# Spreading Bx with two single-pass products, moving the second group of flips, and moving half of the Bx products, in an adapter-plus-experts kernel

## The reference

```
Bx    = einsum('bni,bri->bnr', x, B[itok])          # 512 x 16 per batch
c     = einsum('bnr,bor->bno', Bx, A[itok])         # adapter output
base  = c @ base_w.T + base_b
w     = top2(softmax(c @ router_w.T)), renormalised
delta = einsum('bse,bsr,eor->bso', w, c @ A.T, B)   # 16 experts, rank 64
out   = x + base + 0.5 * delta
```

## Time and profile before

| | before |
|---|---|
| median of 3 runs | 446.18 us |
| lowest and highest | 445.64, 464.56 us |
| the profiled execution | 445.62 us, of it 443.8 us span |
| TensorE busy | 92% of the span |
| VectorE busy | 72% |
| ScalarE busy | 24% |
| GpSimd busy | 9% |
| granted TensorE clock | 0.996 of full speed |

### The profile page before, as it was taken

The page is one execution under the profiler, slowest core; times in us unless marked ns, Lnnn a source line. Parts: engine busy times, 40 slices in busy tenths (PEclk is TensorE's granted clock), DMA queues, the critical chain, the costliest instruction groups (busy, mean ns, idle before and its releaser), DMA issues.

```text
span 443.8 us, 6785 instructions
## 1 busy us (share of the span) xinstructions
PE 409.7 (92%) x2496; PEld 279.9 (63%) x2496; DVE 319.4 (72%) x830; ACT 108.1 (24%) x163; POOL 40.5 (9%) x53
## 2 busy tenths in 40 slices
PE   0597997999788999999999999999999999999996
PEld 0475985656556766666667666666666676666665
DVE  2699996999468496668677875966686778756453
ACT  0003114435473231123113112311231131123110
POOL 4020000002100120012001201200120012012000
PEclk9999998999999999999999999999999999999999
DMA  8999999999999999899999999998999898556935
GB/s 223 357 330 331 334 357 366 345 269 336 289 295 239 352 362 323 279 349 342 310 287 378 306 315 302 366 312 295 348 335 325 285 366 303 207 201 217 343 128 189
DMA packets 75027, 135.35 MB, mean 305 GB/s; under 512 B 5506, under 2 KB 14770, under 8 KB 74994
## 3 DMA queue, kind: packets, MB, share of 16 engines
q1 hardware_dynamic: 56000, 102.08, 69.7%
q10 hardware_dynamic: 18994, 32.84, 23.5%
HBM read 99.23 MB, written 35.65 MB: 304 GB/s over the span
## 4 chain that ended last, share of the span: by engine, by line
PE 63%; DVE 10%; DMA 9%; SPq 6%; POOL 3%; ACT 3%; issue 3%; ACTq 2%; POOLq 0%; DVEq 0%
PE ps L927 13%; PE ps L928 11%; PE ps L929 11%; PE ps L901 11%; PE ps L941 6%; DMA bexpT<-in_x 6%; PE ps L930 5%; POOL u_r L480 3%; DMA gm_r<-xT 3%; DVE xT L728 3%; DVE early L659 3%; SPq L296 3%; ACT bexpT L495 2%; PE ps L856 2%; PE ps L949 2%
## 5 line engine op out<-in xcount | busy, mean ns | idle before, releaser
L840 DVE TENSOR_TENSOR xbuf<-ps,xbuf 128x512 f32<-128x512 f32 x128 | 86.7, 677 | 96.0 <-PE ps L930 96.0
L927 PE MATMUL ps<-h_r,u_r 128*128 128x512 f32 x256 | 108.8, 425 | 0.7
L928 PE MATMUL ps<-h_r,u_r 128*128 128x512 f32 x256 | 100.3, 392 | 0.0
L929 PE MATMUL ps<-h_r,u_r 128*128 128x512 f32 x256 | 100.1, 391 | 0.0
L866 PE MATMUL ps<-early 128*128 128x256 f32 x256 | 66.5, 408 | 22.6 <-DVE early L659 22.6
L728 DVE STREAM_TRANSPOSE xT<-xbuf 128x256 f32<-128x256 f32 x224 | 80.6, 410 | 0.0
L866 PEld LDWEIGHTS ps<-early 128*128 128x128 f32 x256 | 48.1, 201 | 36.8 <-issue 16.5
L927 PEld LDWEIGHTS ps<-h_r,u_r 128*128 128x128 f32 x256 | 48.1, 188 | 35.9 <-issue 16.7
L659 DVE STREAM_TRANSPOSE early<-xbuf 128x256 f32<-128x256 f32 x128 | 65.9, 577 | 5.3 <-issue 3.8
L901 PE MATMUL ps<-bexpT,cur 128*32 128x512 f32 x512 | 61.6, 598 | 2.2 <-DVE h_r L707 1.5
L495 ACT ACTIVATE h_r<-ps 128x512 fp32r<-128x512 f32 x64 | 36.2, 595 | 78.8 <-PE ps L901 78.4
(11 more groups left out here) (67 smaller groups left out, 205.3 us busy)
## 6 DMA issues: line engine op xcount, KB each, us to landing
out<-xbuf SPq DMA_DIRECT2D x31, 1024.0 KB, 7.3
xbuf<-in_x SPq DMA_DIRECT2D x28, 1024.0 KB, 7.4
xbuf<-in_x ACTq DMA_DIRECT2D x32, 512.0 KB, 10.9
xbuf<-in_x SPq DMA_DIRECT2D x32, 512.0 KB, 8.6
xbuf<-in_L_ffn_base_w SPq DMA_DIRECT2D x16, 512.0 KB, 19.3
xbuf<-in_L_ffn_base_w ACTq DMA_DIRECT2D x16, 512.0 KB, 20.1
gm_r<-g_hilo SPq DMA_DIRECT2D x128, 32.0 KB, 6.8
early_u<-in_L_ffn_B SPq DMA_DIRECT2D x10, 256.0 KB, 18.5
```

The lines of the kernel that those rows point to most:

```text
L840: dve.tensor_tensor(xs, ps[:, tile_bank(b.n, m), :], xs, ALU.add).then_inc(s_out, 1)
L927: pe.matmul(acc, u_r[:, b.q, 0, h, tok_t], hi, start=(h == 0), stop=False)
L928: pe.matmul(acc, u_r[:, b.q, 0, h, tok_t], lo, start=False, stop=False)
L929: pe.matmul(acc, u_r[:, b.q, 1, h, tok_t], hi, start=False, stop=False)
```

## The change

Four edits, and one argument of the compiler:

1. The spread of Bx. `spread` is float32r, and Bx is split into a high part `bxs_r[:,0]` (a second ScalarE copy out of `BXB` in slot 8) and a low part `bxs_r[:,1]` (a VectorE subtraction, the first thing in slot 9). Two single-pass products replace the one in 32 bits. They stand in slot 10, behind tile 10, and so do ScalarE's copies of the result.
2. Both groups of flips stand behind tile 13. The multiplications that use them stay in slots 13 and 14.
3. The first half of the Bx products stands ahead of tile 4, directly behind `h_products`, for every front (before: ahead of tile 3, with f = 1 already there).
4. `T_AT` changes: in slot 3 nothing, in slots 4, 5, 6 and 7 two pairs each (four transposes). Before it was two pairs in slot 3, two in 4, one in 5, two in 6, one in 7.
5. `dynamic_dma_scratch_size=1024` makes room for the new tile.

```
-        BX_AFTER = {90: 3, 101: 8}
+        BX_AFTER = {90: 4, 101: 8}
...
-        T_AT = {0: (5, 6), 1: (7,), 3: (8, 9), 4: (10, 11), 5: (12,), 6: (13, 14), 7: (15,)}
+        T_AT = {0: (5, 6), 1: (7,), 4: (8, 9), 5: (10, 11), 6: (12, 13), 7: (14, 15)}
...
-            return {4 if f.n == 1 else 3: range(0, KD), 8: range(KD, 2 * KD)}.get(m, ())
+            return {4: range(0, KD), 8: range(KD, 2 * KD)}.get(m, ())
...
-        CT_AT = UP_AT = {13: 0, 14: 1}
+        REP_AT, CT_AT = 10, 13
+        UP_AT = {13: 0, 14: 1}
...
                     copy(bxp, ps[:, BXB, :]).then_inc(s_bxp, 1)
+                    need(act, s_rep, f.n)
+                    copy(bxs_r[:, 0, :], ps[:, BXB, :]).then_inc(s_bxhi, 1)
...
-                if m == SPREAD_AT:
+                if m == REP_AT:
                     act.wait_ge(s_rep, f.n + 1)
...
                 if m == MAX_AT:
+                    dve.wait_ge(s_bxp, f.n + 1)
+                    dve.wait_ge(s_bxhi, f.n + 1)
+                    dve.tensor_tensor(bxs_r[:, 1, :], bxp, f32(bxs_r[:, 0, :]), ALU.subtract).then_inc(s_bxlo, 1)
                     dve.wait_ge(s_lg, f.n + 1)
...
-                    pe.matmul(ps[:, BXB, :], spread[:, f.q, :], bxp,
-                              start=True, stop=True).then_inc(s_rep, 1)
-                if m in CT_AT:
...
+                if m == REP_AT:
+                    pe.wait_ge(s_bxhi, f.n + 1)
+                    pe.wait_ge(s_bxlo, f.n + 1)
+                    pe.matmul(ps[:, BXB, :], spread[:, f.q, :], bxs_r[:, 0, :], start=True, stop=False)
+                    pe.matmul(ps[:, BXB, :], spread[:, f.q, :], bxs_r[:, 1, :], start=False, stop=True)\
+                      .then_inc(s_rep, 1)
+                if m == CT_AT:
                     pe.wait_ge(s_combk, f.n * 2 + 2)
...
-    nc = bacc.Bacc("TRN2", target_bir_lowering=False, num_devices=1)
+    nc = bacc.Bacc("TRN2", target_bir_lowering=False, num_devices=1, dynamic_dma_scratch_size=1024)
```

More of the change, by code:

```diff
@@ L116, in adaln_ffn @@
         ident = sb("ident", [P, P])
-        spread = sb("spread", [P, 2, P])
+        spread = sb("spread", [P, 2, P], F32R)
+        bxs_r = sb("bxs_r", [P, 2, T], F32R)
         pick = sb("pick", [P, 2, RK])
@@ L178, in adaln_ffn @@
         s_xe, s_bxq = sem("x_transposed"), sem("bx_products")
+        s_bxhi, s_bxlo = sem("bx_partial_hi"), sem("bx_partial_lo")
         s_bxp, s_lg, s_rep, s_bx = sem("bx_partial"), sem("logits"), sem("bx_spread"), sem("bx_copied")
@@ L265, in adaln_ffn, with bx_before @@
         T_AHEAD = {12: (0,), 13: (1,), 14: (2,), 15: (3, 4)}
-        T_AT = {0: (5, 6), 1: (7,), 3: (8, 9), 4: (10, 11), 5: (12,), 6: (13, 14), 7: (15,)}
+        T_AT = {0: (5, 6), 1: (7,), 4: (8, 9), 5: (10, 11), 6: (12, 13), 7: (14, 15)}
         REFILL_AT = {4: 0, 8: 1}
-        def bx_before(f, m):
-            return {4 if f.n == 1 else 3: range(0, KD), 8: range(KD, 2 * KD)}.get(m, ())
+        def bx_before(m):
+            return {4: range(0, KD), 8: range(KD, 2 * KD)}.get(m, ())
         def ring_place(f, j):
@@ L933, in bx_products @@
             def bx_products(f, m):
-                for k in bx_before(f, m):
+                for k in bx_before(m):
                     g, j = k // KD, k % KD
@@ L951, in slot @@
                     ins.then_inc(s_lg, 1)
-                    pe.matmul(ps[:, BXB, :], spread[:, f.q, :], bxp,
-                              start=True, stop=True).then_inc(s_rep, 1)
-                if m in CT_AT:
-                    h = CT_AT[m]
-                    pe.wait_ge(s_combk, f.n * 2 + 2)
[L957 to L962, removed]
+                if m == REP_AT:
[5 more added lines that the diff above has]
+                if m == CT_AT:
+                    pe.wait_ge(s_combk, f.n * 2 + 2)
+                    for h in range(2):
+                        if h == 1:
+                            pe.wait_ge(s_bx, f.n + 1)
+                        for t in range(NT):
+                            w = combk[:, t, h * EH:(h + 1) * EH, :].rearrange("p e k -> p (e k)")
+                            ins = flip((MISC, BXB)[h], t * P, w)
+                        ins.then_inc(s_ct, 1)
             pe.wait_ge(s_masks, 4)
```

## The result

The changed kernel takes 448.61 us in the median of 7 runs (447.69 to 450.61). The kernel before takes 445.64 us in the median of 7. The ratio is 1.0072 with a 95% interval of 1.0051 to 1.0094: slower by 0.7%. That is less than 2%, and the interval leaves out 1. Forecast were 449.1 us, range 444.8 to 452.2. Some executions, whatever the kernel, are disturbed and some per cent longer (one of before at 464.56 us), and the ratios leave them out, as do the medians of the experiments' table.

The account below looks back on a forecast made before the run. TensorE was taken as the bound, unless VectorE's stream is longer between meeting points. Six steps of 0.88 - 0.34 (+3.2), step 0 (-0.34) and the first part (+0.6) add 3.5 to 445.62: 449.1 us, range 444.8 to 452.2.

Parts of the forecast that it names:

- The stretch: VectorE's gapless work from tile 4's add to the last transpose ahead of tile 8: from 7.62 to 8.98 us.
- Tile 8: Its start in steps with f = 2 to 7: 0.88 us later, the 0.46 us saved by the Bx move included.
- The spread: Two single-pass products replace the long one: -0.95 + 0.15 + 0.46 = -0.34 us a step, bounds -0.49 and -0.29.
- The term without a row: First product of tile 10, now behind the logits' short products: 0.15 us extra, bounds nothing and 0.20.
- The cover of the subtraction: Slot 9: the 0.67 us subtraction hides in VectorE's 2.08 us idle ahead of tile 10's add, costing nothing.
- Flips and scratch: Both flip groups behind tile 13: price 0, bounds 0 and +0.2 us; the smaller DMA scratch: 0.
- the first part: Ahead of the steps, the subtraction lies uncovered on VectorE's path: +0.6 us once, bounds 0 and 1.2.
- step 0: Its transposes already had this order, hidden by the expert flips, so only the spread's saving counts: -0.34 us.
- (a): Rival: VectorE keeps up, so only the saved mode changes count: -4.5 us, 441.1 us; chance 0.12.
- (b): Rival: the Bx move saves no change of mode, adding 2.8 us: 451.9 us; chance 0.08.
- (c): Rival: TensorE's new waits lower its clock from 2.4 to 1.2 GHz: 458.8 us; chance 0.03.
- (d): Rival: the spread gives nothing or the wait is half as long, so parts cancel: 446 us; chance 0.12.

Follow-up runs that it names:

- e1: The changed kernel with the kernel before's table of transposes, so two pairs in slot 3 again: 441.13 us, ratio 0.9905 to the kernel before.
- e5: The changed kernel with one pair of transposes put back into slot 3 and the later ones moved up: 444.48 us, ratio 0.9977.
- e9: The changed kernel with one useless VectorE multiplication added in slot 5, between the adds of tiles 4 and 8: 452.66 us, ratio 1.0154.
- e3: The kernel before with only the first half of the Bx products moved ahead of tile 4 and the new table of transposes: 450.92 us, ratio 1.0114.
- e2: The changed kernel with Bx products and transposes placed as before, so new spread and flips alone: 444.42 us, ratio 0.9967.
- e6: The changed kernel with the old table of transposes and the subtraction for Bx's low part on GpSimd instead of VectorE: 440.59 us, ratio 0.9881.
- e4: The kernel before with both groups of flips behind tile 13 and the smaller DMA scratch: 445.13 us, ratio 0.9993.
- e7: The changed kernel with the old table of transposes and the flips apart again, behind tiles 13 and 14: 440.97 us, ratio 0.9891.
- e8: The changed kernel with one useless VectorE multiplication added in slot 3, where VectorE is idle: 448.71 us, ratio 1.0063.

## Why the prediction was right

**The direction and the mechanism.** The step that decided was edit 4, the four transposes put into a stretch without gaps. e1 shows it by taking it away, e5 by halving it, e9 by lengthening the stretch with other work. The three periods lie within 0.04 us of what was expected of each.

**Its terms, against the trace of after.** The time from tile 0's first load to tile 4's add fell from 219.59 - 206.99 = 12.60 us to 12.13. The second is 219.78 less 207.65, which is the same load of step 2 in the changed kernel, one period of 41.10 before that of step 3. That is 0.47 saved, forecast 0.46. The stretch is 228.71 - 219.78 = 8.93 us, forecast 8.98. From the last transpose to tile 8's load it is 229.31 - 228.71 = 0.60, forecast 0.61. Tile 8 thus starts 0.81 us later than before in a step, forecast 0.88, and e3 alone measures 0.78.

**The spread.** Forecast -0.34, measured -0.35 in e2. The term without a row, the first product of tile 10 behind the logits, was taken as 0.15 over the plain 0.23. The chain after shows 0.33, so 0.10 over. The two products cost 0.23 each, as forecast. So the parts add up to -0.95 + 0.10 + 0.46 = -0.39, and the agreement of -0.34 with e2's -0.35 is in part luck: where the other 0.04 goes wasn't looked for.

**The cover of the subtraction was thinner than I said.** The prediction set it against the 2.08 us that VectorE idled ahead of tile 10's add. It left out that the long spread had also held tile 10 back, so that the change shortens the cover from both sides, by 0.60 for the subtraction and by 0.85 for the tile. What is left is 0.62 us. The subtraction is still hidden, as e6 shows. A second one, which nobody tried, would use up nearly all that is left.

**Flips and scratch.** Priced at 0. e4 measures 0 for both, e7 for the flips.

**The sum.** Six steps of 0.54 were forecast, six of 0.41 measured: 3.2 against 2.5 us. This is the term that was too large: tile 8 is later by 0.81 and not 0.88, and the spread's parts give 0.39 and not 0.34. The terms for the first part (+0.6) and step 0 (-0.34) make +0.26. Each can be seen, at the first load of tile 0 of step 0, before and after:

```profile
116.32 0.19 PEld L927 LDWEIGHTS ps<-h_r,u_r 128*128 128x128 f32 x1 [0.84 <-issue]
```

```profile
116.89 0.19 PEld L935 LDWEIGHTS ps<-h_r,u_r 128*128 128x128 f32 x1 [0.84 <-issue]
```

The first part is 0.57 us longer. At 97.54 VectorE starts the maximum in before, and the subtraction in the changed kernel, where the maximum follows at 98.11, also 0.57 later. One pair of traces does not prove it: e4 without the subtraction and e7 with it both have this load at 115.67. From this load to the mark at the end of step 0 it is 164.98 - 116.32 = 48.66 before and 165.19 - 116.89 = 48.30 after, so -0.36. Here all traces agree: 48.66 to 48.70 in before, e3 and e4, and 48.30 to 48.35 in the kernels with the new spread. So the two terms give +0.21, and each of them came close to its forecast. One term was not in the sum at all: an execution is longer than its span by 1.8 us in before, e3 and e4, and by 2.1 in all kernels with the new spread. These 0.3 us are in the 3.0 that the changed kernel lost, and what makes them was not tried.

**The rivals.** (a), VectorE keeps up, would have given 441.1 us. It was wrong for this kernel, and it is what e1 measures once the transposes have their old place. (b), the move saves no change of mode, is refuted by the 0.47 us, and by the 0.48 between e1 and e2. (c), a lower clock, did not come: the row of slices is as before, and the granted clock is 1.00 in each of the steps with the new wait. (d), cancelling parts, is what happens in kind, but the wait was its full size.

## What to carry to other kernels

A move that saves time on the bounding engine is worth what it saves only if the helper that feeds it keeps its place in time: look for the stretch between two meeting points where the helper has no gap, and count what the edit puts into it. Idle time of a helper is worth something only ahead of the point where the stretch begins, and 25% of idle in the period says nothing about it. When an edit bundles parts, price each with its own sign: here the new table of transposes alone cost 1.7% (from e1 to the changed kernel) and hid that all the rest gained 0.95%.

## What the runs showed of the hardware that I had not expected

Kernels that are alike in the first part and step 0 but for small edits reach the end of step 0 at different times. The difference is made before the first load of tile 0, which stands between 115.67 (e4, e7) and 118.03 us (e2); from there to the mark it is 48.5 us within 0.2 in all. e4, which is before with other flips, has the mark at 164.36 us and before has it at 164.98. e7 is e1 with other flips and has it at 164.02, e1 at 165.19; e2 is the latest with 166.33. In e2 the wait for the load of x into `bexpT` was 4.1 us against 3.5 before, and the clock row has two slices below 9 instead of one. The granted clock from 70 to 80 us of the span goes with it in the main. It is 1.00 in e4, e7 and e8, whose marks are 164.02 to 164.79, and 0.83 in before, the changed kernel, e1, e3, e5, e6 and e9, with marks from 164.75 to 165.51. In e2 it is 0.66, and from 74 to 80 us it is 0.50, the lower of the two levels (1.2 GHz). Ahead of that stretch TensorE waits for transposes of `base_w`: 1.62 us in e7, 2.09 in e4, 2.86 in before and 3.46 in e2. The length of this wait alone does not settle it, since e8 kept its clock behind 2.37 us and e6 lost it behind 2.08. These are single executions, and no run changed the clock alone. The five periods that follow, from the end of step 0 to that of step 5, repeat within 0.06 us in each kernel. So a per-step price can be read to a few hundredths from one trace, while the total of one trace carries an error of about a microsecond. Of e2's microsecond over its expectation, 0.3 are also those outside the span.
